# Two of six row sums per batch tile: four partial sums on TensorE, the rest on VectorE

## What is computed

```python
e = jnp.stack([tbl_0[ids[:, 0]], ..., tbl_31[ids[:, 31]]], axis=1)   # (1024, 32, 16)
x0 = xk = e
for W in (W0, W1, W2):                     # (32, 32, 64), (32, 64, 64), (32, 64, 64)
    xk = jax.nn.relu(jnp.einsum('bmd,bhd,mhk->bkd', x0, xk, W))
    outs.append(jnp.sum(xk, axis=2))       # the sum over d, 16 numbers each
z = jnp.concatenate(outs, axis=1)          # (1024, 192)
h = jnp.concatenate([z, dense_ctx], axis=1)
h = jnp.maximum(h @ W_top1 + b_top1, 0.0)  # (208, 512)
h = jnp.maximum(h @ W_top2 + b_top2, 0.0)  # (512, 256)
y = h @ W_top3                             # (1024, 1)
```

## Time and profile before

| | us |
|---|---|
| three runs | 682.65, 685.11, 689.90 (median 685.11) |
| the profiled execution, its own time | 682.96 |
| its span in the trace (first to last instruction) | 681.1 |
| PE busy in the span | 601.3 (88%) |
| DVE busy | 580.6 (85%) |
| POOL busy | 502.3 (74%) |
| ACT busy | 353.1 (52%) |

### The profile page before, as it was taken

How to read it: one execution, slowest core, us unless ns; L and a number is a source line. 1 busy time by engine, 2 the same in 40 slices (tenths; PEclk the granted TensorE clock), 3 DMA queues, 4 the chain that set the end, 5 groups by cost and what they waited for, 6 DMA issues and landing times. The chain is left out here.

```text
span 681.1 us, 9217 instructions
## 1 busy us (share of the span) xinstructions
PE 601.3 (88%) x3394; PEld 218.2 (32%) x3394; DVE 580.6 (85%) x541; ACT 353.1 (52%) x550; POOL 502.3 (74%) x360
## 2 busy tenths in 40 slices
PE   4112687999999998999999999999999999999998
PEld 3001641222223422343224322432243223433344
DVE  7000927899999998999999999999999999989993
ACT  0000026745467546666666656754675467646851
POOL 6773004495998889888888898889888987666670
PEclk9999988999999998999999999999999999999999
DMA  5120299979934996299729991899089916992000
GB/s 126 22 23 3 57 233 242 227 141 227 233 66 57 244 222 150 33 231 212 198 24 202 218 229 13 178 227 251 8 163 238 242 30 131 241 215 73 1 2 1
DMA packets 89040, 95.96 MB, mean 141 GB/s; under 512 B 59830, under 2 KB 67795, under 8 KB 88995
## 3 DMA queue, kind: packets, MB, share of 16 engines
q1 hardware_dynamic: 78594, 91.23, 60.9%
q0 software_dynamic: 7552, 1.95, 3.0%
q10 hardware_dynamic: 2848, 2.18, 1.1%
HBM read 91.92 MB, written 3.94 MB: 141 GB/s over the span
## 5 line engine op out<-in xcount | busy, mean ns | idle before, releaser
L934 DVE TENSOR_TENSOR z<-xk,x0rep 128x1024 f32<-128x1024 f32 x460 | 525.9, 1215 | 33.4 <-ACT xk L733 12.0
L650 PE MATMUL acc<-z,w_sb 128*64 128x512 f32 x1840 | 437.6, 599 | 17.8 <-DVE z L934 15.1
L482 POOL TENSOR_TENSOR z_pool<-x0rep,xk_copy 128x1024 f32<-128x1024 f32 x116 | 275.7, 2379 | 100.2 <-DMA x0rep<-x_rows 52.3
L429 POOL DMA_INDIRECT emb<-tbl,idx x236 | 225.9, 957 | 62.1 <-issue 57.1
L650 PEld LDWEIGHTS acc<-z,w_sb 128*64 128x64 f32 x1840 | 124.3, 137 | 298.1 <-issue 170.1
L761 ACT ACTIVATE xk<-xk_copy 32x1024 f32<-32x1024 f32 x128 | 130.4, 1019 | 96.4 <-DVE z L934 86.9
L650 PE MATMUL acc<-z_pool,w_sb 128*64 128x512 f32 x464 | 119.5, 593 | 0.0
L772 ACT ACTIVATE xk_copy<-acc 64x512 f32<-64x512 f32 x128 | 75.2, 588 | 2.4 <-PE acc L650 1.2
L892 DVE TENSOR_TENSOR x0rep<-xk,line_of 125x1280 f32<-125x1280 f32 (+1 forms) x20 | 26.1, 1373 | 51.8 <-PE xk L577 51.8
L595 PE MATMUL acc<-x0rep 125*32 125x128 f32 (+1 forms) x368 | 23.4, 318 | 50.6 <-issue 50.6
L754 ACT ACTIVATE xk<-lay 128x1024 f32<-128x1024 f32 x16 | 16.4, 1028 | 82.8 <-DVE z L934 45.2
(11 more groups left out here) (54 smaller groups left out, 124.5 us busy)
## 6 DMA issues: line engine op xcount, KB each, us to landing
x0rep<-x_rows SPq DMA_DIRECT2D x128, 512.0 KB
lay<-x_rows SPq DMA_DIRECT2D x32, 512.0 KB
emb<-tbl,idx POOLq DMA_INDIRECT x236
squares<-x_rows SPq DMA_DIRECT2D x16, 128.0 KB
x_rows<-emb SPq DMA_DIRECT2D x7, 256.0 KB
x_rows<-emb SPq DMA_DIRECT2D x9, 128.0 KB
w_wrap<-w ACTq DMA_DIRECT2D x4, 128.0 KB, 3.0
w_sb<-w ACTq DMA_DIRECT2D x8, 64.0 KB
```

Of the source, the lines that this page charges most:

```text
L429: pool.indirect_dma_start(out=emb[:, i % 2, m, :], out_offset=None, in_=tables[m], in_offset=bass.IndirectOffsetOnAxis(ap=idx[:, i, m:m + ...
L482: pool.tensor_mul(z_pool[:, (count - 1) % POOL_RING, :], x0rep[:, g % X0_GROUPS, slot, :], xk_copy[:, side, :]).then_inc(z_pool_ready, 1)
L650: mm = pe.matmul(bank[c * H:(c + 1) * H, :], w[:, tile, :], src[:, c * COLS:(c + 1) * COLS], start=(k == 0), stop=last)
L934: dve.tensor_mul(z[:, (count - 1) % RING, :], xk[:, bank, :], src).then_inc(z_ready, 1)
```

## The change

In the five phases (i,2,Bs) with i = 1 to 5 the two sums over d are made in two parts. PE first adds the 16 values of d in fours: for each of the two outputs it multiplies `layer_out` by the identity four times, each time with every fourth column (128 columns, 16 bytes apart), accumulating into a 128x128 area of `top`, in two halves of 64 output partitions. That is eight `pe.matmul` calls for each output, sixteen for each phase. They stand ahead of step k = 10, behind a wait until the dense network's last output of the tile before has been taken from `top`. DVE then reduces 128 columns (32 rows by 4) from `top` in place of 512 from `layer_out`. Its two reductions move from behind c = 7 and 9 to behind c = 11 and 12, and both wait on a new semaphore until both outputs of the pair have been added.

```diff
+ADDED_FIRST = [n for n, ph in enumerate(PHASES) if ph[1:] == (2, Bs) and 0 < ph[0] < NT - 2]
+ADD_AT = 10
+FOURS = D // 4
+ADD_COUNT = {ph: c + 1 for c, ph in enumerate(ph for n in ADDED_FIRST for ph in SUMS[n])}
 def sums_after(n, k):
-    at = {1: (8,), 2: (7, 9)}[len(SUMS[n])] if n in SUMS else ()
+    at = {1: (8,), 2: (7, 9) if n not in ADDED_FIRST else (11, 12)}[len(SUMS[n])] if n in SUMS else ()
     return [SUMS[n][at.index(k)]] if k in at else []
...
+        def added_at(phase):
+
+            at = (ADD_COUNT[phase] - 1) % 2 * ROWS * FOURS
+            return top[:, at:at + ROWS * FOURS]
...
+            def add_fours(phase):
+
+                n = NUMBER[phase]
+                pe.wait_ge(acc_taken, n + 1)
+                fours = layer_out[:, n % OUTS, :].rearrange("p (r f) -> p r f", f=4)
+                for f in range(4):
+                    for half in range(2):
+                        op = pe.matmul(added_at(phase)[halves[half], :], ident_f[:, halves[half]], fours[:, :, f],
+                                       start=(f == 0), stop=(f == 3))
+                op.then_inc(added, 1)
...
+                    if n in ADDED_FIRST and k == ADD_AT:
+
+                        pe.wait_ge(unit_taken, 3 * i)
+                        for phase in SUMS[n]:
+                            add_fours(phase)
...
-                dve.wait_ge(acc_taken, n + 1)
-                dve.tensor_reduce(row_sums[:, i % 2, SUM_ROWS.index((layer, side)), :],
-                                  layer_out[:, n % OUTS, :].rearrange("p (b d) -> p b d", d=D), AX_X, ALU.add
+                if phase in ADD_COUNT:
+
+                    dve.wait_ge(added, -(-ADD_COUNT[phase] // 2) * 2)
+                    rows = added_at(phase).rearrange("p (b f) -> p b f", f=FOURS)
+                else:
+                    dve.wait_ge(acc_taken, n + 1)
+                    rows = layer_out[:, n % OUTS, :].rearrange("p (b d) -> p b d", d=D)
+                dve.tensor_reduce(row_sums[:, i % 2, SUM_ROWS.index((layer, side)), :], rows, AX_X, ALU.add
                                   ).then_inc(reduced, 1)
```

More of the change, by code:

```diff
@@ L267, in build @@
         reduced = sem("reduced")
+        added = sem("added")
         cleared = sem("cleared")
```

## The result

Over 20 runs each the changed kernel takes 688.54 us in the median (685.76 to 693.35), the kernel before 686.35 us (682.65 to 690.20). The ratio is 1.0045, with an interval of 1.0026 to 1.0065: slower by 0.45%, 3.1 us. The forecast was 683.0 us, faster by 1.2. The measured time lies inside the range, on the other side of no change.

A forecast was written before the change was run, and what follows sets the result against it. DVE was taken to bound the steady tiles at 70.3 us. Three phases at 0.4 us gave 1.2 us: 681.8 by the profiled run, 683.9 by the median, so 683.0 was forecast, range 680.3 to 690.3.

The forecast's parts named there:

- What bounds the kernel: Steady tiles: DVE sets the pace at 70.3 us, PE needs 67.3 and starves behind k = 10 of phase 24.
- Removed from and added to DVE: Each of five phases: two 512-column reductions go, 1.18 us of DVE's queue; two of 128 columns come, 0.44 us.
- Added to PE: Sixteen 128-column products a phase, priced at 1.74 us from L518's row, whose columns lack the 16-byte step; 8.7 us in all.
- The argument that a half does not read a new column in every cycle: Against the slow strided read: a PE step costs 0.84 ns a column, two cycles at 2.4 GHz, which may leave room.
- The prediction's own sign of being wrong: In the profile after: adds over 2.2 us, DVE slice waits in phases 25, 31 or 37, or PE no longer starving.
- The added wait: DVE behind c = 11, until PE has added both outputs: 0.33 us a phase, 0 to 0.7 allowed.
- the rival: Strided read at twice the price: adds 3.5 us, DVE's wait 2.1, 5.2 us slower, 688.2 to 690.3; chance 0.17.
- Net for one tile: Where DVE sets the pace: 1.18 - 0.44 - 0.33 = 0.41, so 0.4 us gained a tile (0 to 0.8).
- Where it counts: Phases 24, 30 and 36 count, 1.2 us together; in 12 and 18 later waits for x0 slices hide the gain.
- the 0.74 us that it adds for PE's lag in phase 18: Phase 18: PE reaches k = 10 3.62 us behind the pair's start against 2.88 in phase 24, so DVE waits 0.74 longer.
- the second rival: Slice loads, not DVE, set the tile's length, so no change: 682.96 or 685.1 us; chance 0.20, shared with gain eaten.
- The chances: Forecast 0.55, gain hidden or eaten 0.20, strided read to about double 0.17, dearer 0.08; within 1% of no change 0.88.

The follow-up runs named there:

- the half-slice kernel: Kernel before, loading half of each x0 slice from (1,0,Bs) on, the other half stale; 629.14 us, ratio 0.9812 to the whole-slice kernel before.
- adding in twos: The change with PE reading 256 columns 8 bytes apart twice per output and DVE reducing 256; ratio to before 0.9967, in a repeat 0.998.
- a whole-slice kernel of the second set: The change with ACT writing layer_out of the added phases in PE's reading order, sums over d kept; ratio to before 1.0002.
- the kernel with tiles 1 and 2 alone: The change in phases 12 and 18 only, with phases 24, 30 and 36 as before; ratio to the kernel before 0.9976 (0.9946 to 1.0006).

## Why the prediction was wrong

*What bounds the kernel.* DVE sets the tile at 70.30 us, and PE starves behind k = 10: right, in the half-slice kernel to the hundredth. "From 321 to 575 us DVE waits once" was true of one execution and was read as true of the kernel. In other executions slices are waited for in other tiles.

*Removed from and added to DVE.* Right: 0.20 us in the queue for a reduction, 0.22 forecast.

*Added to PE.* This is the step that failed: "I take 1.74, the nearest row in shape." It measured 3.61, and with side-by-side columns and all else equal 1.75. The row had the shape and not the step between columns. The upper bound of 3.5 us, given from nothing but a factor of two, came close. The argument that a half does not read a new column in every cycle, and may have room, fell: such room, if there is any, did not cover columns 16 bytes apart. The prediction's own sign of being wrong, adds over 2.2 us, was met.

*The added wait.* The working was right and inherited the wrong term. With columns side by side the wait is 0.26 us (0.33 forecast; its terms add to 0.35), with the strided read 2.15 (2.1 in the rival).

*Net for one tile.* 0.4 us forecast, 0.44 with the right products and nothing else in the way; -1.44 as the change stands, where the rival had -1.33.

*Where it counts.* Phase 12 cost nothing and phase 18 0.5 us, where the rival's sum has 1.2: the 0.74 us that it adds for PE's lag in phase 18 did not come, the wait there was 2.14 us as in phase 24. The sum also left out the 1.0 us that the last slice's wait gave back. The step that phases 24, 30 and 36 count in full, because DVE has no wait for slices in phases 25, 31 and 37, was wrong too, though it did not turn the sign: with whole slices a saving of 4.1 us on DVE left at most 2.5. So the second rival, the hidden gain, was in part true beside the first. With half slices the change costs 7.2 to 8.0 us, with whole ones 3.1 us were measured; that the slices cover the difference fits their waits, 7.0 us before and 3.6 after, but these are one profile each, and other whole-slice kernels waited 2.5 to 13.5 us in stretches of 450 to 460 us.

*The chances.* The rival that came true had 0.17 and a time of 688.2 to 690.3; the median was 688.54. Its mechanism was right and its time partly luck: it adds 5.2 us, and 3.1 were measured, but the kernel before has a median of 686.35 us over 20 runs where the prediction reckoned from 682.96 and 685.11. The forecast of 683.0 lies low for the same reason. The case for the rival (a read pattern that no row shows) was in the prediction and was given too little weight beside a row alike in all else.

What stays open: how much of the spread between runs is the slices' landing and how much the clock in the first 110 us; whether adding in twos is worth anything, up to 0.5%; and why PE was late with the adds at k = 7 and whole slices. Phases 24, 30 and 36 were not tried alone; that they hold the loss follows from the table and from the kernel with tiles 1 and 2 alone.

## What to carry to other kernels

A price read from a row holds for the access pattern of that row: float32 columns 16 bytes apart cost PE twice those side by side (3.61 against 1.75 us), and 8 bytes apart 3% more (1.81). Splitting a sum in twos, or letting an engine with time to spare write the order in which PE will read, avoids the price, though neither was shown to make this kernel faster. Work moved off the engine that sets the pace comes back if that engine then has to wait for the result; place it early enough that the result is there when it is asked for, even if it takes longer than reckoned. Where loads land just in time, a profile without waits for them does not say that there is slack; take the loads away once, and see.

## What had not been expected

The kernel before took 687.81 us in the first set of experiments and 640.85 and 638.33 us in the other two. Of these 47 us 45.5 lie at the start: the second sum begins at 138.98 us in the first profile of before and at 93.51 in a whole-slice kernel of the second set. In the first profile PE's small products of the lookup (L595) come one by one, with the engine waiting for nothing that the profile shows:

```profile
18.30 0.37 PE L595 MATMUL acc<-x0rep 125*32 125x128 f32 x1 [1.74 <-issue]
19.70 0.37 PE L595 MATMUL acc<-x0rep 125*32 125x128 f32 x1 [1.03 <-issue]
21.79 0.37 PE L595 MATMUL acc<-x0rep 125*32 125x128 f32 x1 [1.72 <-issue]
```

In a profile of the second set the same products stand close, 72 in 4.49 us:

```profile
12.57 4.49 PE L619 MATMUL acc<-x0rep 125*32 125x128 f32 x72 [5.40 <-DVE x0rep L925]
```

Nothing in the kernels differs there. Up to 110 us, PE's weight loads for these products wait 56.9 to 58.1 us for nothing that the profile shows in both profiles of the result and all four of the first set, and 6.2 to 10.5 us in all eight of the other two sets. So the wait goes with the set and not with the kernel; the three sets ran on three different chips, and chip and time cannot be told apart here. What makes PE wait was not tried; it changes nothing in the tiles, where unchanged pairs stand 70.30 us apart in the first profile and in the half-slice one of the second set.
